# L2's attention layer: stores in two parts, one running maximum, and diagonals by ScalarE

## The chip, the cores and the metric

One Trainium2 chip, one of its cores. The metric is the device time of one execution in microseconds, and of several runs the median. The engines are named as in the profile: PE (TensorE, with PEld for its weight loads), DVE (VectorE), ACT (ScalarE), POOL (GpSimd) and SP (SyncE, which here only issues transfers).

## What is computed

Four pairs of a graph layer and a feed-forward layer, each added to a residual x of 3125 nodes by 256 features; the graph has 50000 edges. The stages that the change touches most belong to the third graph layer, L2:

```python
def _L2_gnn_ref(feature, src, dst, W_s, W_t, W_attn, W_fc, b_fc):
    proj_s = feature @ W_s.T
    proj_t = feature @ W_t.T
    z = proj_s[src] + proj_t[dst]
    z = jnp.where(z >= 0, z, NEG_SLOPE * z)
    e = (z @ W_attn.T)[:, 0]
    m = jax.ops.segment_max(e, src, num_segments=n)
    e_exp = jnp.exp(e - m[src])
    denom = jax.ops.segment_sum(e_exp, src, num_segments=n)
    alpha = e_exp / denom[src]
    agg = jax.ops.segment_sum(feature[src] * alpha[:, None], dst, num_segments=n)
    return agg @ W_fc.T + b_fc
```

So the softmax is over the edges that leave a node, and the sum over the edges that enter one: two passes over the edges, the first sorted by source, the second by destination.

## The kernel before, in words

The nodes lie in 25 windows (T) of 125 rows (PT), one node per partition. The edges, padded and sorted by window, lie in 415 tiles (NTE) of 128. Each engine runs a hand-written program in order; semaphores (`Mark`, and `Ring` for transfers that take turns) order the engines against each other, and at the end of each stage `K.meet` makes all five wait for one another. The stages of L2 are these.

L2Project makes the projections window by window. SP stores each window into tables in HBM: tabT (257 columns, line 2305) and tabB (386 columns, line 2309), each a transfer of 125 rows. At the end SP waits for the landings (line 2316).

L2Max is the pass by source. POOL gathers one tile of tabT rows per instruction (line 2543), which it may do 16 tiles ahead; a buffer comes free with PE's sum of its tile and with ACT's copy of its last column (line 2598). PE sums into PSUM (lines 2632, 2634); DVE forms the score of each edge (line 2563) and per group of four tiles adds the gathered part to it (line 2571). Then it multiplies the identity by the four score columns (line 2577), which gives four diagonal matrices of 128x128. PE multiplies these by ones, on top of a mask of which edge belongs to which node (lines 2614, 2616, in `lay`), so that a bank holds the scores of a group laid out by node. DVE takes the maximum of each tile and node (line 2547) into TM, negates it (line 2553), and ACT forms the sum of exponentials against it (line 2606) into TS. Once per eight tiles DVE also compares a row of 1024 edge positions with the partition number (line 2493).

L2Combine lies between the passes. TM and TS hold, per node, one maximum and one sum for each of 415 tiles, though a tile belongs to one window only. For each of 25 windows DVE compares the window number of all tiles with it (line 2669), adds that as a penalty and takes the maximum (line 2678, over 415 columns), ACT forms 415 exponentials (line 2708), and DVE sums them against TS (line 2698). Small DVE steps make the scale and the shift of the normalised features (lines 2673 to 2691), ACT writes them into a row buffer (lines 2714 to 2717), and SP stores them into the last 258 columns of tabB (line 2722), again 125 rows at a time. POOL clears the accumulator of the next stage (line 2660). PE has no part in it.

L2Sum is the pass by destination; its first instruction on POOL is a gather of tabB (line 2756).

The other tables are stored in the same way: tabA in the sort (line 599) and for L1 (line 1862), whose landing SP waits for; tabC in L3Project (line 2933, landing at line 2935), where DVE clears an accumulator at the end (line 2956); and the output (line 3373).

Of the kernel before, what the change touches and what calls it, by code (L numbers as in the profile page):

```python
# [18 lines left out]
D = 256  # L19
T = 25  # L20
# [62 lines left out]
class Kit:  # L83
# [94 lines left out]
    def dma(self, total=1, keep=False, kind="dma"):  # L178
        return self.mark(total, 16, keep, kind)

    def ring(self, slots, total, kind="dma", keep=False):

        return Ring([self.dma((total - r + slots - 1) // slots, keep, kind) for r in range(min(slots, total))])
# [324 lines left out]
class Sort:  # L508
# [8 lines left out]
    def __init__(self, K):  # L517
# [38 lines left out]
        self.tab, self.got = K.ring(4, T), K.dma()  # L556
# [38 lines left out]
    def sync_tables(self, s, edges):  # L595
        K = self.K
        for t in range(T):
            s.wait_ge(*self.stored.n(t + 1))
            s.dma_start(K.tabA[t * PT:(t + 1) * PT, :], self.acc[0:PT, t * D:(t + 1) * D]).then_inc(*self.tab.up(t))
# [566 lines left out]
class Moe:  # L1166


    def __init__(self, K, layer, E, top, F, NT, key, router, rbias, ecols, shared=False, post=None, side=None):
# [88 lines left out]
        if layer == 0:  # L1258
            self.table = K.W(T * D)
            self.c_norm, self.c_out = K.mark(T), K.ring(4, T)  # L1260
# [597 lines left out]
    def table_sync(self, s):  # L1858
        K = self.K
        for t in range(T):  # L1860
            s.wait_ge(*self.c_norm.n(t + 1))
            s.dma_start(K.tabA[t * PT:(t + 1) * PT, :], self.table[0:PT, t * D:(t + 1) * D]).then_inc(*self.c_out.up(t))
# [381 lines left out]
class L2Project(Project):  # L2244
# [4 lines left out]
    def __init__(self, K, source):  # L2249
# [23 lines left out]
        self.got, self.tabT, self.tabB = K.dma(), K.ring(self.RT, T), K.ring(self.RS, T)  # L2273
# [23 lines left out]
    def sync(self, s):  # L2297
# [4 lines left out]
        for i in range(T + 3):  # L2302
            if i < T:
                s.wait_ge(*self.score.n(i + 1))
                s.dma_start(K.tabT[i * PT:(i + 1) * PT, :], self.whole(i, 1)).then_inc(*self.tabT.up(i))
            if i >= 3:
                t = i - 3
                s.wait_ge(*self.part[2].n(2 * t + 1))
                s.dma_start(K.tabB[t * PT:(t + 1) * PT, 0:DP], self.psB[0:PT, t % self.RS * DP:(t % self.RS + 1) * DP]).then_inc(*self.tabB.up(t))
# [195 lines left out]
class L2Max:  # L2505
# [49 lines left out]
    def vector(self, v):  # L2555
# [3 lines left out]
        for k in range(NTE):  # L2559
# [5 lines left out]
            if k % 4 == 3 or k == NTE - 1:  # L2565
# [76 lines left out]
class L2Combine:  # L2642


    def __init__(self, K, proj):
# [3 lines left out]
        self.pen = [g(EP) for _ in range(4)]  # L2649
        self.ex = [g(EP) for _ in range(3)]  # L2650
        self.jk = g(EP)
        self.row = [g(D + 2) for _ in range(4)]
        self.scale, self.shift = g(32), g(32)
        self.maxes, self.expo, self.sums = K.mark(T), K.mark(T), K.mark(T)
        self.scales, self.filled = K.mark(T), K.mark(T)
        self.cleared = K.mark(1)
        self.out = K.ring(4, T)

    def gpsimd(self, g):
        g.memset(self.pr.acc[0:PT, :], 0.0).then_inc(*self.cleared.up)  # L2660
        g.wait_ge(*self.cleared.n(1))

    def vector(self, v):
        K, pr, own = self.K, self.pr, self.K.own_v
        for i in range(T + 4):
            if i < T:
                if i >= 4:
                    v.wait_ge(*self.expo.n(i - 3))
                v.tensor_scalar(self.pen[i % 4][0:PT, 0:NTE], K.wtS[0:PT, 0:NTE], float(i), -BIG, ALU.not_equal, ALU.mult).then_inc(*own.up)
            if 4 <= i:  # L2670
                t = i - 4
# [1234 lines left out]
```

## Time and profile before

| | us |
|---|---|
| median of 3 runs | 5704.95 |
| lowest and highest of them | 5691.93, 5708.81 |
| the profiled execution, time | 5709.71 |
| its span, first to last instruction | 5707.6 |
| L2Max, first gather to last exponential | 2786.0 to 3340.7 |
| L2Combine, up to the first gather of L2Sum | 3340.9 to 3402.85 |
| busy in the span: PE, DVE, ACT, POOL | 4446.5, 3468.2, 2051.0, 3554.7 |

Times in rows are microseconds from the start of the span unless marked ns. A tile name such as small or big is the memory that the buffers were cut from; "bank" is PSUM. "x25" is a count of instructions, and what stands behind "|" or in brackets is idle time of that engine before them and what ended it. In the tables by stretch the order is: from and to, length, busy time of PE, PEld, DVE, ACT and POOL with counts, the granted clock of PE as a share of full speed (1.00 is 2.4 GHz, 0.50 is 1.2), the share of the 16 DMA engines that was busy, and GB/s.

### The profile page before, as it was taken

To read this page: it belongs to the slowest core of one execution; us is meant where nothing else is said; L and a number is where in the kernel's file an instruction comes from. 1 tells how busy PE (TensorE), PEld (TensorE's weight loads), DVE (VectorE), ACT (ScalarE), POOL (GpSimd) and SP (SyncE) were. 2 spreads that over 40 slices of the span, in tenths; PEclk is the share of its full clock that TensorE was granted. 3 is DMA by queue.
4 is the path that set the end of the run, shared out by engine and by line. 5 is a ranking of instruction groups with operands and counts; after the bars stand their busy time and mean duration, and the time that the engine had idled before them with its cause. 6 is when DMAs were issued, how large, how long until landed. Compare 5 with 4: busy or idle time off the path is not lost. (4 is left out here: it accounts for less than half of the span.)

```text
span 5707.6 us, 86269 instructions
## 1 busy us (share of the span) xinstructions
PE 4446.5 (78%) x19702; PEld 2875.8 (50%) x19702; DVE 3468.2 (61%) x12030; ACT 2051.0 (36%) x7165; POOL 3554.7 (62%) x3817
## 2 busy tenths in 40 slices
PE   6958787799867777387599848888696788877768
PEld 4423337699723335344355526666594333345536
DVE  8957543310167774524466668887415688867775
ACT  7900002233333334023333345554243455544331
POOL 7777775677567773674677737775124477756620
PEclk8955658899856668556899979999696899999978
DMA  2543346688567771142344438886473588876500
GB/s 61 161 153 103 105 102 195 230 274 273 193 182 205 207 202 21 53 106 72 106 128 128 127 99 278 287 278 193 149 211 110 152 231 231 229 186 190 157 19 23
DMA packets 531878, 914.75 MB, mean 160 GB/s; under 512 B 99410, under 2 KB 381985, under 8 KB 522945
## 3 DMA queue, kind: packets, MB, share of 16 engines
q0 software_dynamic: 161600, 449.89, 28.3%
q1 hardware_dynamic: 309354, 330.73, 18.6%
q10 hardware_dynamic: 60438, 128.64, 7.3%
q8 instruction: 186, 3.05, 0.2%
q14 instruction: 300, 2.45, 0.1%
HBM read 739.18 MB, written 169.72 MB: 159 GB/s over the span
## 5 line engine op out<-in xcount | busy, mean ns | idle before, releaser
L1132 PE MATMUL bank<-small 128*125 128x256 f32 x1660 | 818.5, 614 | 302.2 <-DVE small L1099 163.8
L1080 POOL DMA_INDIRECT small<-tabA,idxD x830 | 803.4, 968 | 267.2 <-issue 181.3
L1132 PEld LDWEIGHTS bank<-small 128*125 128x125 f32 x1660 | 372.9, 277 | 747.0 <-issue 409.1
L3018 POOL DMA_INDIRECT small<-tabC,idxD x415 | 410.3, 989 | 190.9 <-SPq L202 64.8
L914 POOL DMA_INDIRECT recs<-pkS,rowS x391 | 385.6, 986 | 229.5 <-issue 98.2
L2756 POOL DMA_INDIRECT big<-tabB,idxD x415 | 395.0, 952 | 198.4 <-issue 88.9
L2543 POOL DMA_INDIRECT big<-tabT,idxS x415 | 411.7, 992 | 138.5 <-issue 107.5
L1111 DVE TENSOR_TENSOR big<-big,bank 125x256 f32 x830 | 347.6, 419 | 240.9 <-PE bank L1132 224.6
L1665 DVE COPY small<-bank 128x256 f32<-128x256 f32 x176 | 74.8, 425 | 680.5 <-PE bank L1720 680.5
L3096 PE MATMUL bank<-big,cst 128*125 128x512 f32 x830 | 427.2, 596 | 0.5 <-ACT big L3083 0.5
L1709 PE MATMUL bank<-small,big 128*128 128x128 f32 (+1 forms) x3040 | 400.2, 288 | 0.0
L1720 PE MATMUL bank<-big 128*128 (+1 forms) x1520 | 390.9, 404 | 3.1 <-issue 3.1
L1709 PEld LDWEIGHTS bank<-small,big 128*128 128x128 f32 (+1 forms) x3040 | 368.1, 196 | 19.0 <-issue 18.9
L3082 ACT ACTIVATE big<-cst,small 128x128 f32<-128x128 f32 x830 | 286.9, 393 | 241.0 <-DMA small<-tabC,idxD 237.8
L1633 POOL DMA_INDIRECT small<-tabA,small x176 | 169.0, 960 | 311.4 <-PE bank L1696 160.6
L3177 POOL TENSOR_TENSOR big<-big 128x256 f32<-128x256 f32 x415 | 245.7, 630 | 144.8 <-ACT big L3238 144.8
L3264 PE MATMUL bank<-big,small 128*125 128x260 f32 x830 | 268.1, 423 | 65.5 <-DVE big L3217 60.8
L2406 PE MATMUL bank<-big,small 125*128 x1245 | 214.4, 281 | 133.6 <-DMA big<-tabB,idxD 72.0
L1720 PEld LDWEIGHTS bank<-big 128*128 128x128 f32 (+1 forms) x1520 | 286.8, 199 | 52.0 <-issue 21.5
L1749 ACT ACTIVATE big<-bank,small 128x128 f32<-128x128 f32 (+1 forms) x760 | 220.8, 367 | 245.9 <-PE bank L1709 241.8
L1121 ACT ACTIVATE small<-small 128x256 f32<-128x256 f32 x415 | 172.9, 417 | 373.4 <-DVE small L1104 373.4
L3065 DVE TENSOR_REDUCE small<-bank 125x4 f32<-125x512 f32 x415 | 284.1, 685 | 0.0
(495 smaller groups left out, 10440.9 us busy)
## 6 DMA issues: line engine op xcount, KB each, us to landing
big<-in_L_w ACTq DMA_DIRECT2D x56, 1024.0 KB
small<-eaS SPq DMA_DIRECT2D x415, 128.0 KB
eaS<-small SPq DMA_DIRECT2D x415, 128.0 KB, 2.8
big<-eaS SPq DMA_DIRECT2D x415, 128.0 KB, 3.1
big<-in_L2f_w ACTq DMA_DIRECT2D x64, 512.0 KB
big<-rowsD SPq DMA_DIRECT2D x104, 256.0 KB, 3.9
ytab<-small ACTq DMA_DIRECT2D x176, 128.0 KB
big<-rowsS SPq DMA_DIRECT2D x52, 256.0 KB
```

What stands on the lines that cost most here:

```text
L914: g.indirect_dma_start(out=K.recs, out_offset=bass.IndirectOffsetOnAxis(ap=K.rowS[:, c:c + 1], axis=0), in_=K.pkS[:, c:c + 1], in_offset=N ...
L1080: g.indirect_dma_start(out=self.gb[k % self.RG], out_offset=None, in_=K.tabA, in_offset=row_index(K.idxD, k)).then_inc(*self.got.up(k))
L1111: v.tensor_tensor(rows, rows, K.bank[k % 4][0:PT, 0:D], ALU.add).then_inc(*self.added.up)
L1132: p.matmul(self.K.bank[k % 4][0:PT, 0:D], self.oh[k % self.RO][:, 0:PT], self.gb[k % self.RG], start=True, stop=True).then_inc(*self.summe ...
L1709: m = p.matmul(self.hidden(k, hf)[0:hc, j * 128:j * 128 + 128], w1[:, c * F + f * 128:c * F + f * 128 + hc], xT[:, c, :], start=(c == 0), ...
L1720: m = p.matmul(K.bank[6 + k % 2][:, 0:D], self.hT[k % self.RT][0:hc, f * 128:(f + 1) * 128], K.big[0:hc, bass.ds(where + f * D, D)], start ...
L2543: g.indirect_dma_start(out=self.rows(k)[:, 0, :], out_offset=None, in_=K.tabT, in_offset=row_index(K.idxS, k)).then_inc(*self.got.up(k))
L2756: g.indirect_dma_start(out=self.gb[k % self.RB], out_offset=None, in_=K.tabB, in_offset=row_index(K.idxD, k)).then_inc(*self.got.up(k))
L3018: g.indirect_dma_start(out=self.gb[k % self.RG], out_offset=None, in_=K.tabC, in_offset=row_index(K.idxD, k)).then_inc(*self.got.up(k))
L3065: v.tensor_reduce(self.tm[k % 4][0:PT, 0:4], K.bank[k % L][0:PT, :].rearrange("p (h e) -> p h e", h=4), AXX, ALU.max).then_inc(*self.top.up)
L3082: a.activation(self.diagonals(k, h, 1), K.ident, ACT.Copy, scale=gb[:, D + h:D + h + 1])
L3096: p.matmul(b, K.ones[:, 0:PT], self.dg[k % self.RD], start=False, stop=True).then_inc(*self.field.up)
```

## The change

Stores: the new `store_rows` issues rows 0 to 111 and rows 112 to 124 as two transfers, and the marks that count landings count 32 in place of 16. It is used for tabA (both), tabT, tabB, tabC and the output.

L2Max: the diagonals of a group are made by ACT, with four copies of the identity that are scaled by a score column, in place of DVE's one multiplication. ACT does this after it has freed the buffers of the next group and before the exponentials.

L2Combine is written anew. The tiles of a window stand side by side in sorted order, so DVE runs one maximum along the 415 tiles that starts again where the window changes; its value at the last tile of each window is the window's maximum. PE picks these values by transposes and matmuls with 0/1 matrices (`of`: tile belongs to window, made by POOL; `last`: it is the last of it). PE spreads the maxima back over the tiles, DVE subtracts, ACT forms one exponential over 415 columns, DVE multiplies by TS, and PE sums by window in the same way. The normalised features are written by DVE and ACT, three and two of each five windows, and stored five windows at a time.

```diff
+def store_rows(s, dst, src, landed):
+    s.dma_start(dst[0:112], src[0:112]).then_inc(landed[0], 16)
+    s.dma_start(dst[112:PT], src[112:PT]).then_inc(landed[0], 16)
...
@@ L2Max.vector
                 if g >= self.LR:
                     self.highest(v, g - self.LR)
-                if g >= self.RD:
-                    v.wait_ge(*self.field.n(g - self.RD + 1))
-                v.wait_ge(*self.whole.n(g + 1))
-                v.tensor_tensor(self.dg[g % self.RD][:, 0:n * 128].rearrange("p (t e) -> p t e", e=128), K.ident.unsqueeze(1).broadcast_to([128, n, 128]),
-                                pr.Ecol[:, four].unsqueeze(2).broadcast_to([128, n, 128]), ALU.mult).then_inc(*self.spread.up)
@@ L2Max.scalar
+            if 1 <= g <= NG:
+                self.spread_terms(a, g - 1)
             if g >= self.LE:
...
+    def spread_terms(self, a, g):
+        K, pr = self.K, self.pr
+        if g >= self.RD:
+            a.wait_ge(*self.field.n(g - self.RD + 1))
+        a.wait_ge(*self.whole.n(g + 1))
+        for i in range(self.size(g)):
+            k = 4 * g + i
+            ins = a.activation(self.dg[g % self.RD][:, 128 * i:128 * i + 128], K.ident, ACT.Copy, scale=pr.Ecol[:, k:k + 1])
+        ins.then_inc(*self.spread.up)
@@ L2Combine
+    NB, P, WR = 4, 104, D + 2
...
     def gpsimd(self, g):
+        K = self.K
+        g.tensor_scalar(self.of[0:T, 0:NTE], K.wtS[0:T, 0:NTE], K.lane[0:T, 0:1], None, ALU.is_equal).then_inc(*self.marked.up)
         g.memset(self.pr.acc[0:PT, :], 0.0).then_inc(*self.cleared.up)
...
     def vector(self, v):
...
+        v.memset(self.flag, 1.0).then_inc(*own.up)
+        v.wait_ge(*own.all)
+        v.tensor_tensor(self.flag[:, 1:NTE], K.wtS[:, 1:NTE], K.wtS[:, 0:NTE - 1], ALU.not_equal).then_inc(*self.flagged.up)
+        v.wait_ge(*self.flagged.n(1))
+        v.tensor_scalar(self.reset, self.flag, -4.0 * BIG, None, ALU.mult).then_inc(*own.up)
+        v.wait_ge(*own.all)
+        v.tensor_tensor_scan(out=self.run[0:PT, 0:NTE], data0=self.reset[0:PT, 0:NTE], data1=TM, initial=-4.0 * BIG,
+                             op0=ALU.add, op1=ALU.max).then_inc(*self.ran.up)
+        v.wait_ge(*self.marked.n(1))
+        v.tensor_tensor(self.last[0:T, 0:NTE], self.of[0:T, 0:NTE], self.flag[0:T, 1:NTE + 1], ALU.mult).then_inc(*self.turned.up)
...
+        v.tensor_tensor(self.less[0:PT, 0:NTE], TM, K.bank[4][0:PT, 0:NTE], ALU.subtract).then_inc(*self.lowered.up)
+        v.wait_ge(*self.expo.n(1))
+        v.tensor_tensor(self.ex[0:PT, 0:NTE], self.ex[0:PT, 0:NTE], TS, ALU.mult).then_inc(*self.weighed.up)
...
+        for t in range(T):
+            if t % 5 % 2 == 0:
+                v.tensor_scalar(self.rows[0:PT, t, 0:D], K.xt(t), self.scale[0:PT, t:t + 1], self.shift[0:PT, t:t + 1],
+                                ALU.mult, ALU.add).then_inc(*self.filled_v.up)
...
+    def tensor(self, p):
...
+        p.wait_ge(*self.turned.n(1))
+        for b in range(self.NB):
+            n, at = self.size(b), b * 2 * T
+            p.transpose(K.bank[0][0:n, at:at + T], self.of[0:T, b * P:b * P + n], K.ident[0:T, 0:T])
+            m = p.transpose(K.bank[0][0:n, at + T:at + 2 * T], self.last[0:T, b * P:b * P + n], K.ident[0:T, 0:T])
...
+        for b in range(self.NB):
+            n = self.size(b)
+            m = p.transpose(K.bank[(1, 7)[b // 2]][0:n, b % 2 * 128:b % 2 * 128 + PT], self.run[0:PT, b * P:b * P + n], K.ident[0:PT, 0:PT])
...
+        for b in range(self.NB):
+            n, at = self.size(b), b * 2 * T + T
+            p.matmul(K.bank[3][0:T, 0:PT], self.pick[0:n, at:at + T], self.runT[0:n, 128 * b:128 * b + PT], start=(b == 0), stop=(b == self.NB - 1))
+        for b in range(self.NB):
+            n, at = self.size(b), b * 2 * T + T
+            m = p.matmul(K.bank[2][0:PT, 0:T], self.runT[0:n, 128 * b:128 * b + PT], self.pick[0:n, at:at + T], start=(b == 0), stop=(b == self.NB - 1))
...
+        p.matmul(K.bank[4][0:PT, 0:NTE], self.MT[0:T, 0:PT], self.of[0:T, 0:NTE], start=True, stop=True).then_inc(*self.wide.up)
...
     def sync(self, s):
...
+        for q in range(5):
+            s.wait_ge(*self.filled_a.n(2 * q + 2))
+            s.wait_ge(*self.filled_v.n(3 * q + 3))
+            store_rows(s, K.tabB.rearrange("(t p) d -> p t d", p=PT)[:, 5 * q:5 * q + 5, DP:DP + D + 2],
+                       self.rows[0:PT, 5 * q:5 * q + 5, :], self.out.up)
```

The matmul and transpose groups each wait for the copies out of PSUM before them and raise a mark behind them; the last two groups (four transposes of `ex`, four matmuls by `of`) have the form of those shown.

## Rows read from the trace of the kernel before

**Rows 1.** By stretch: length, busy us of PE, PEld, DVE, ACT, POOL

```profile
2900.00:3000.00 100.00, 90.28 (x290) 52.21 (x288) 65.38 (x246) 31.31 (x172) 76.41 (x78) 1.00 0.49 129
...
3341.00:3403.00 62.00, 0.00 (x0) 0.00 (x0) 52.30 (x225) 33.07 (x100) 5.51 (x2) 0.50 0.18 52
```

**Rows 2.** The page's group of L2Max's gathers; busy us, mean ns

```profile
L2543 POOL DMA_INDIRECT big<-tabT,idxS x415 | 411.7, 992 | 138.5 <-issue 107.5
```

**Rows 3.** Line 2543: ns min/median/max, and one cause of idling

```profile
L2543 POOL DMA_INDIRECT big<-tabT,idxS x415: 942/946/1447, 2786.0 to 3322.9; - x139
...
  PE bank L2634: 16.1, 53
```

**Rows 4.** Timeline in L2Max: start, length; a lengthened gather, then an undisturbed one

```profile
2999.53 0.68 DVE L2577 TENSOR_TENSOR small<-cst,big 128x512 f32<-128x512 f32 x1
2999.58 1.45 POOL L2543 DMA_INDIRECT big<-tabT,idxS  x1 [0.30 <-issue]
...
3005.08 0.94 POOL L2543 DMA_INDIRECT big<-tabT,idxS  x1 [0.30 <-issue]
...
3005.58 0.68 DVE L2577 TENSOR_TENSOR small<-cst,big 128x512 f32<-128x512 f32 x1
```

**Rows 5.** Groups of instructions by line in L2Combine: count, busy us, mean ns

```profile
L2708 ACT ACTIVATE small<-small,big 125x415 f32<-125x415 f32 x25 | 16.0, 641 | 23.2 <-DVE big L2687 23.2
L2678 DVE CUSTOM_DVE_ANT_0 small<-big,small 125x415 f32<-125x415 f32 x25 | 14.8, 591 | 0.9
L2717 ACT ACTIVATE small<-X,small 125x256 f32<-125x256 f32 x25 | 14.6, 586 | 0.0
...
L2687 DVE TENSOR_SCALAR big<-big 125x1 f32<-125x1 f32 x25 | 3.9, 154 | 0.9
```

**Rows 6.** Timeline at the start and at the end of L2Combine

```profile
3340.90 5.96 DVE L2669 TENSOR_SCALAR small<-wtS 125x415 f32<-125x415 f32 x2 [3.18 <-ACTq L204]
3340.92 5.43 POOL L2660 MEMSET big<- 125x6400 f32 x1 [17.06 <-PEq L204]
...
3402.85 0.95 POOL L2756 DMA_INDIRECT big<-tabB,idxD  x1 [56.49 <-SPq L202]
```

**Rows 7.** What SP's queue waited for: us in total, times, longest

```profile
SPq L2935 <- DMA tabC<-big: 7.4, 1, 7.4
SPq L2316 <- DMA tabB<-big: 6.0, 3, 2.7
...
SPq L1009 <- DMA tabA<-big: 4.5, 1, 4.5
```

**Rows 8.** By stretch; the last two numbers are DMA share and GB/s

```profile
4470.00:4475.00 5.00, 5.00 (x29) 4.17 (x28) 2.03 (x5) 3.22 (x10) 0.00 (x0) 1.00 0.35 107
...
3412.00:3436.00 24.00, 19.56 (x126) 13.79 (x125) 18.04 (x81) 11.10 (x32) 17.08 (x19) 0.93 0.89 294
```

**Rows 9.** Timeline at the end of L3Project

```profile
4476.34 5.47 DVE L2956 MEMSET big<- 125x6500 f32 x1 [1.30 <-issue]
```

**Rows 10.** Timeline in L3Max: two ACT copies of a scaled diagonal

```profile
4699.62 0.69 ACT L3082 ACTIVATE big<-cst,small 128x128 f32<-128x128 f32 x2 [1.02 <-DMA small<-tabC,idxD]
```

**Rows 11.** Groups by line and shape: POOL's operations and DVE's scan

```profile
L819 POOL TENSOR_SCALAR small<-big 128x125 f16<-128x125 f16 x78 | 59.7, 786 | 10.2 <-DVE big L618 8.6 <-PE bank L719 1.6
...
L1782 POOL TENSOR_TENSOR X<-X,big 125x1280 f32<-125x1280 f32 x5 | 14.4, 2889 | 5.1 <-ACT big L1892 5.0
...
L425 DVE TENSOR_TENSOR_SCAN big<-big 128x391 f16<-128x391 f16 x50 | 48.9, 1017 | 0.0
```

**Rows 12.** PE at half clock: a stretch, then two rows of the timeline

```profile
2785.00:2788.00 3.00, 1.95 (x8) 1.52 (x8) 0.00 (x0) 0.13 (x1) 1.66 (x2) 0.50 0.12 26
...
2796.90 2.08 PE L2632 MATMUL bank<-big,cst 128*128 128x512 f32 x2 [9.13 <-DVE big L2493]
...
2797.92 0.34 PEld L2634 LDWEIGHTS bank<-big 125*128 125x128 f32 x1 [0.52 <-issue]
```

**Rows 13.** What the exponentials of line 2606 waited for (us, times)

```profile
  DVE big L2553: 44.5, 46
```

More of the change, by code:

```diff
@@ L176, in mark, with dma, ring @@
         return m
[L178 to L183, printed above, removed]
+    def dma(self, total=1, keep=False, kind="dma", parts=1):
+        return self.mark(total, 16 * parts, keep, kind)
+    def ring(self, slots, total, kind="dma", keep=False, parts=1):
+        return Ring([self.dma((total - r + slots - 1) // slots, keep, kind, parts) for r in range(min(slots, total))])
     def close(self):
@@ L2648, in __init__, with size @@
         K.w_at, K.g_at = proj.w_end, 0
[L2649 to L2652, printed above, removed]
+        self.flag, self.reset, self.run, self.of, self.last = g(EP), g(EP), g(EP), g(EP), g(EP)
+        self.less, self.ex = g(EP), g(EP)
+        self.pick, self.runT, self.exT = g(self.NB * 2 * T), g(self.NB * 128), g(self.NB * 128)
+        self.M, self.MT = g(32), g(128)
         self.scale, self.shift = g(32), g(32)
-        self.maxes, self.expo, self.sums = K.mark(T), K.mark(T), K.mark(T)
-        self.scales, self.filled = K.mark(T), K.mark(T)
+        self.rows = K.big[:, 0:T * self.WR].rearrange("p (t c) -> p t c", c=self.WR)
+        self.flagged, self.marked, self.turned, self.picks = K.mark(1), K.mark(1), K.mark(1), K.mark(1)
+        self.ran, self.flipped, self.back_a, self.back_v = K.mark(1), K.mark(1), K.mark(1), K.mark(1)
+        self.most, self.kept, self.wide = K.mark(1), K.mark(1), K.mark(1)
+        self.lowered, self.expo, self.weighed = K.mark(1), K.mark(1), K.mark(1)
+        self.flipped2, self.back_a2, self.back_v2, self.summed = K.mark(1), K.mark(1), K.mark(1), K.mark(1)
+        self.scaled, self.filled_a, self.filled_v = K.mark(1), K.mark(10), K.mark(15)
         self.cleared = K.mark(1)
-        self.out = K.ring(4, T)
+        self.out = K.dma(5, parts=2)
+    def size(self, b):
+        return min(self.P, NTE - b * self.P)
     def gpsimd(self, g):
+        K = self.K
+        g.tensor_scalar(self.of[0:T, 0:NTE], K.wtS[0:T, 0:NTE], K.lane[0:T, 0:1], None, ALU.is_equal).then_inc(*self.marked.up)
         g.memset(self.pr.acc[0:PT, :], 0.0).then_inc(*self.cleared.up)
@@ new lines, in scalar @@
+    def scalar(self, a):
+        K, pr, w = self.K, self.pr, 128 * self.NB // 2
+        a.wait_ge(*self.picks.n(1))
+        a.activation(self.pick[0:self.P, :], K.bank[0][0:self.P, 0:self.NB * 2 * T], ACT.Copy).then_inc(*K.own_a.up)
+        a.wait_ge(*self.flipped.n(1))
+        a.wait_ge(*K.own_a.all)
+        a.activation(self.runT[0:self.P, w:2 * w], K.bank[7][0:self.P, 0:w], ACT.Copy).then_inc(*self.back_a.up)
+        a.wait_ge(*self.most.n(1))
+        a.activation(self.rows[0:PT, :, D], K.bank[2][0:PT, 0:T], ACT.Copy, scale=-1.0).then_inc(*K.own_a.up)
+        a.activation(self.rows[0:PT, :, D + 1], K.bank[2][0:PT, 0:T], ACT.Copy).then_inc(*K.own_a.up)
+        a.wait_ge(*self.lowered.n(1))
+        a.activation(self.ex[0:PT, 0:NTE], self.less[0:PT, 0:NTE], ACT.Exp).then_inc(*self.expo.up)
+        a.wait_ge(*self.flipped2.n(1))
+        a.activation(self.exT[0:self.P, w:2 * w], K.bank[0][0:self.P, 0:w], ACT.Copy).then_inc(*self.back_a2.up)
+        a.wait_ge(*self.scaled.n(1))
+        a.wait_ge(*K.own_a.all)
+        for t in range(T):
+            if t % 5 % 2:
+                a.activation(self.rows[0:PT, t, 0:D], K.xt(t), ACT.Identity, scale=self.scale[0:PT, t:t + 1],
+                             bias=self.shift[0:PT, t:t + 1]).then_inc(*self.filled_a.up)
@@ L2727 @@
+    def sync(self, s):
+        K = self.K
+        for q in range(5):
[3 more added lines that the diff above has]
+                       self.rows[0:PT, 5 * q:5 * q + 5, :], self.out.up)
+        s.wait_ge(*self.out.all)
 class L2Sum:
@@ L3359, in __init__ @@
         self.w_flip, self.w_turn, self.w_out, self.done = (K.mark(T) for _ in range(4))
-        self.stores = K.ring(8, T)
+        self.stores = K.ring(8, T, parts=2)
     def sync(self, s):
@@ L3732, in _ @@
             K.meet(p, "p")
+            l2_comb.tensor(p)
             K.meet(p, "p")
```

116 lines of the change are left out of this document (49 added, 67 removed).

## Prediction

> **What bounds the kernel now.** The kernel is a row of stages, each closed by a meeting of all engines, so a saving inside a stage counts only if it lies on the chain that ends that stage. I read the busy time by stage first. In the diagonal stage (L2's first pass, L2Max, 2786 to 3341 us) PE is busy 90% and POOL 77% of a stretch; in the stage of maxima between the passes (L2Combine, 3341 to 3403 us) PE does nothing and DVE is busy nearly throughout [rows 1]. Next the gathers of L2Max: 415 of them, 0.946 us in the median, and what stands before them is only the 0.3 us of issue; even the pauses put down to PE are 16.1 us in 53 cases, again 0.3 us each [rows 2, 3]. So POOL never waits for a free buffer, and L2Max lasts as long as 415 gathers at 0.946 + 0.30 us (517 us) plus their lengthening, a start and a tail. PE's 90% fits into that. The mean gather is 992 ns, though [rows 2], so lengthened gathers cost 415 x 0.046 = 19.1 us of this bound.
>
> The timeline shows by what. A gather that starts just after the DVE multiplication that builds four diagonals (L2577, 0.68 us) takes 1.45 us; it ends late by about the rest of that instruction. When the multiplication starts half a microsecond into a gather, it costs nothing [rows 4]. Going through the whole stage, 30 gathers of this kind are 9.2 us too long; nearly all of the remaining 10 us fall to the wide comparison L2493, which stays. I read this as two engines needing one way into the memory.
>
> L2Combine is DVE work: 25 window tiles with two 415-column reductions of 0.59 us and a comparison each, and small steps between [rows 5]. Its first DVE comparison lasted until POOL's memset of 5.43 us was over, and the first gather of the next stage comes 61.95 us after the start [rows 6].
>
> Last, what SP waits for at the ends of stages: 7.4 us for tabC, three waits of 6.0 us together for tabB, 4.5 us for tabA [rows 7]. While tabC is stored, the DMA engines stand at a share of 0.35, a little over 5 of 16, and move 107 GB/s; in another stretch they move 294 GB/s at 0.89 [rows 8]. A store of 125 rows thus seems to fill five engines and leave eleven idle.
>
> **Part 1, the stores.** Each store becomes two issues of some 0.25 to 0.4 us on SP. The 112 rows can go out over 16 engines. L3Project: landing ends 7.4 us after the last issue; with little queued it should take 2.5 to 3. DVE's memset, which ends at 4481.8, takes over as the last piece [rows 9], so 4.5 us are gained. L2Project: of the 6.0 us about 2.4 (three more issues are added, and index work on DVE stands close behind). The table of L1: of 4.5 us about 2.1. The other stores of the list lie beside work that is longer (in the sort, edge rows are scattered for long after the last table store): nothing. Sum 9 us, bounds 3 and 13. The pages would give the same direction: the Trainium skill, "DMA: Bandwidth & Descriptors", section on why a DMA increments its semaphore by 16, says that a transfer is spread over the largest number up to 16 that divides its outer dimension, 5 for 125, 16 for 112 and 13 for 13. By that rule the trace's share of 0.35 is what five engines and some noise give.
>
> **Part 2, diagonals by ScalarE.** DVE loses 104 multiplications of 0.68 us. DVE was not the bound, so that by itself is nothing. ACT gets 415 copies of 128x128; two in a row take 0.69 us in a later stage of this kernel [rows 10], so a group of four is about 1.3 us. ACT was busy 32 of 100 us, and a group takes some 5.1 us, so it rises to about 58%. Behind the new wait for the sums of group g-1 stand four exponentials and the freeing of the buffers of the next group; those sums are made a group earlier, and the buffers have four groups of slack, so I cost the wait at nothing. If that cover is gone, see the slow rival. PE needs the diagonals of a group only two groups later. What it does bring is the port: the 9.2 us fall away, less what the other comparison may catch instead. I take 8 us; bounds 0 (the comparison takes over all) and 12. At the tail DVE gains 0.55 us and ACT has three copies to do first: nothing.
>
> Against this stands a page: the Trainium skill, "SBUF — State Buffer", section "Who interferes with whom", says that a DVE operation with two SBUF inputs holds only the shared read interface, and infers from it that such an operation does not stall the making of descriptors. By that remark this part would be worth 0 and the sum 30 us; the 1.45 us gather speaks against it, and it is the first rival.
>
> **Part 3, L2Combine.** Removed: all of the 62 us. Added, from the start t0 = 3340.9:
> POOL compares 415 columns before its memset. From 2.89 us for 1280 columns that is 0.94 us, from the 0.79 us of a comparison over 125 columns 2.6 us [rows 11]; I take 1.6. The memset (5.43) then ends at 7.0. DVE's full-width multiplication by -4 BIG is of the kind that lasted as long as the memset did [rows 6], so I let it end 0.4 after it: 7.4. Scan, as 1.0 us for 391 columns [rows 11], and the marks of last tiles, 0.5: 9.0. PE at half clock, since it has been idle (clock 0.50 in the stretch of 62 us [rows 1]): 12 transposes at 0.21 to 0.25 us each, by 8 in 1.95 us [rows 12]: 11.9. Copies out of PSUM with handoff 0.5: 12.4. Eight fp32 matmuls are 16 records; a weight load is 0.34 at this clock, one record of 512 columns 1.04 [rows 12]; eight records with 25-column weights at 0.25 and eight with 125-column weights at 0.34 are 4.7: 17.1. Copy 0.3, the wide matmul (2 x 0.84 + 0.34) 2.0: 19.4. Subtraction 0.59, exponential 0.64, product 0.59 [rows 5] and handoffs: 21.4. Four transposes 1.1, copies 0.5, eight records 3.0: 26.0. Four small DVE steps on 25 columns, where one on a single column is 0.15 [rows 5], about 0.25 each: 27.0. Then 25 tiles are normalised, 15 by DVE and 10 by ACT; at 0.5 us ACT's ten are 5 us (0.586 is the length of one [rows 5], and they overlap a little). The first five are ready at 28.2. From there 25 x 129 KB = 3.2 MB go out; five engines at 107 GB/s make 342 for sixteen, and 294 was seen [rows 8], so 9.5 to 11 us plus 1.5 us of start: 40. Meeting and issue 0.5: 40.5 against 61.95, a gain of 21 us. The chain is serial, so nothing hides it. Bounds: if the memset holds nobody and PE finds its full clock, 5 + 6 us less, gain 32; if each of some 17 handoffs costs 0.3 more and the stores run at 200 GB/s, gain 10.
>
> **The sum.** 9 + 8 + 21 = 38 us. The profiled execution has a span of 5707.6 and a time of 5709.7; its changed counterpart would take 5671.7. It stands 4.8 us above the median of the runs, so the median 5704.95 becomes 5667.
>
> **Rivals.**
> (a) The gathers are not freed: another DVE instruction catches them instead, or the multiplication was not the cause. For it: the comparison L2493 already takes 10 us of lengthening, and its place relative to the gathers may shift. Against: the lengthened gather of [rows 4] fits the end of the multiplication. 9 + 21 = 30 us: 5675.
> (b) The change doesn't do what it says for the stores: the two parts still run at the old rate, for want of HBM writes or because the small part of 13 rows is slow. Then L2Combine's 3.2 MB at 107 GB/s take 30 us after 28.2, which ends near 60: no gain there and none at the other ends, only part 2 remains. 5697, within 0.3% of before. Against: 294 GB/s were moved elsewhere [rows 8].
> (c) L2Combine's chain is slower than summed, at its bound of 10: 9 + 8 + 10 = 27 us: 5678.
> (d) Slower: ACT becomes the clock of L2Max. It works in order, so a late sum holds four copies, four exponentials and the freeing of buffers. If a group took 0.6 us longer than POOL's 5.1, 104 groups cost 62 us against a gain of 30: 5737. It decides from where ACT's work per group (0.2 + 1.3 + 1.4) plus its waits passes 5.1 us, so waits of over 2.2 us per group would be needed; now its exponentials wait for DVE about 1 us in 46 of the 104 groups [rows 13].
>
> **How the numbers follow.** Forecast 0.58, (a) 0.2, (c) 0.13, (b) 0.06, (d) 0.03. The predicted time is the forecast's, 5667. Its bounds add to gains of 13 to 57 us, but not all ends come together; gains of 18 to 53 hold 8 in 10 with (a) and (c) inside: 5652 to 5687. About 0.3%, or 17 us, is what a measurement can tell from no change. Faster by more: 0.91; within: 0.06; slower: 0.03.
>
> **What would show it.** In the changed profile: L2Combine from the last exponential of L2Max to the first gather of tabB some 41 us, with DVE's full-width multiplication ending just after POOL's memset, and the DMA share near 0.9 in its last 10 us; gathers of L2Max with a mean near 970 ns and still only issue pauses; ACT busy about 58% there; the wait for tabC at 2 to 3 us. I am wrong if POOL in L2Max begins to wait for PE or ACT, if the stores show a share of 0.35 again, or if PE's matmuls in L2Combine take twice what rows at half clock say.

## The result, and the profile after

The changed kernel takes 5652.04 us in the median of four runs (5645.28 to 5656.55); the kernel before, run beside it, takes 5701.41 (5691.93 to 5708.81). The ratio is 0.991 with a 95% interval of 0.9897 to 0.9923, so the change is worth 51 us, between 44 and 59, where 38 were forecast. (Gains in us are worked out below in the same way, from the ratio and its interval.) The direction came as forecast, and so did the gains of the diagonals and of L2Combine, nearly step by step. The stores were worth about twice their term, and with that the median stands at the lower edge of the stated range (5652 to 5687).

The profiled execution of after took 5645.28 us, 7 below its median, and that of before 5709.71, 8 above its own. Their difference of 64.4 us therefore overstates the gain, and below I compare stages across several executions where a few us matter.

L2Max first. The page's group of its gathers answers to [rows 2], the one-line view of its gathers to [rows 3], and the stretch of 100 us to the first row of [rows 1] (order: from and to, length, busy PE, PEld, DVE, ACT, POOL, granted clock, DMA share, GB/s):

```profile
L2549 POOL DMA_INDIRECT big<-tabT,idxS x415 | 404.9, 976 | 136.4 <-issue 104.8 <-PE bank L2647 18.0 <-SPq L202 10.3
```

```profile
L2549 POOL DMA_INDIRECT big<-tabT,idxS x415: 942/946/1392, 2770.8 to 3300.9; - x139
```

```profile
2900.00:3000.00 100.00, 89.94 (x292) 53.46 (x293) 56.14 (x221) 53.34 (x250) 76.23 (x79) 1.00 0.48 130
```

The mean gather fell from 992 to 976 ns, with the median where it was. DVE gave up 9 us per 100 and ACT took on 22. POOL's waits before a gather are again 0.3 us each, also the 59 that are put down to PE (18.0 us): ACT did not become the clock. From the first gather to the last are 530.1 us, against 536.9 before. What is left over 946 ns, 12.5 us in all, falls to gathers beside the comparison that builds 1024 edge positions, here one of them:

```profile
3097.74 0.75 DVE L2499 TENSOR_SCALAR big<-big,lane 128x1024 f32<-128x1024 bf16 x1
3097.91 1.39 POOL L2549 DMA_INDIRECT big<-tabT,idxS  x1 [0.31 <-issue]
```

L2Combine next, from the timeline (start, length, engine, line). It now takes 38.2 us, from 3317.90 to 3356.06, against 61.95 [rows 6]:

```profile
3317.90 1.33 POOL L2684 TENSOR_SCALAR small<-wtS,lane 25x415 f32<-25x415 f32 x1 [16.06 <-ACTq L204]
...
3319.02 5.83 DVE L2695 TENSOR_SCALAR small<-small 128x416 f32<-128x416 f32 x1
3319.19 5.42 POOL L2685 MEMSET big<- 125x6400 f32 x1
3324.88 1.02 DVE L2697 TENSOR_TENSOR_SCAN small<-small,big 125x415 f32<-125x415 f32 x1
...
3326.52 0.25 PE L2753 MATMUL bank<-cst,small 25*104 25x25 f32 x1 [13.01 <-DVE small L2700]
...
3329.16 1.83 PE L2765 MATMUL bank<-small 104*25 104x125 f32 x8 [0.61 <-DVE small L2702]
...
3333.17 1.74 PE L2771 MATMUL bank<-small 25*125 25x415 f32 x2 [0.37 <-DVE small L2704]
...
3341.38 5.02 ACT L2744 ACTIVATE big<-X,small 125x256 f32<-125x256 f32 x10 [3.08 <-DVE small L2718]
3341.38 4.93 DVE L2723 TENSOR_SCALAR big<-X,small 125x256 f32<-125x256 f32 x15
3342.53 0.32 SPq L227 DMA_DIRECT2D tabB<-big  x1
...
3356.06 1.03 POOL L2823 DMA_INDIRECT big<-tabB,idxD  x1 [31.45 <-SPq L202]
```

This is the forecast chain: POOL's comparison, the memset beside a DVE multiplication that lasts until it is over, the scan, PE's short blocks with handoffs of 0.4 to 0.6 us between them, the normalising up to 3346.4, beside which the stores begin, and then nearly 10 us in which nothing but the stores runs. Three stretches, from PE's blocks to the end:

```profile
3330.00:3345.00 15.00, 7.47 (x27) 5.20 (x25) 6.37 (x20) 4.85 (x12) 0.00 (x0) 0.50 0.10 29
3345.00:3350.00 5.00, 0.00 (x0) 0.00 (x0) 1.31 (x5) 1.40 (x3) 0.00 (x0) 0.50 1.02 305
3350.00:3356.00 6.00, 0.00 (x0) 0.00 (x0) 0.00 (x0) 0.00 (x0) 0.00 (x0) 0.50 0.72 212
```

PE works at a granted clock of 0.50, its lower level of 1.2 GHz, as it did when idle before. From 3345 to 3350 the stores fill the DMA engines, at 305 GB/s.

Last, what SP waits for (us in total, times, longest), the answer to [rows 7]:

```profile
SPq L202 <- DMA tabB<-big: 3.9, 1, 3.9
...
SPq L2322 <- DMA tabB<-big: 1.9, 2, 1.4
SPq L3002 <- DMA tabC<-big: 1.2, 1, 1.2
SPq L3442 <- DMA out_x<-X: 1.0, 1, 1.0
SPq L1015 <- DMA tabA<-big: 0.9, 1, 0.9
```

The landing of tabC took 7.4 us and now takes 1.2, those of tabB 6.0 and now 1.9, that of tabA 4.5 and now 0.9. The first line is the new stage's own store.

### The profile page after: what moved, and what is told of

Same layout as the page of the kernel before. It is cut to its first block and busy times, and to the rows that moved or that the text cites. A ratio compares the mean times of both kernels' runs of the same rounds, so it can differ in the third digit from the quotient of the medians.

```text
span 5643.2 us, 86482 instructions
## 1 busy us (share of the span) xinstructions
PE 4436.4 (79%) x19744; PEld 2874.0 (51%) x19744; DVE 3377.0 (60%) x11730; ACT 2141.2 (38%) x7496; POOL 3551.8 (63%) x3818
## 5 line engine op out<-in xcount | busy, mean ns | idle before, releaser
L1715 PEld LDWEIGHTS bank<-small,big 128*128 128x128 f32 (+1 forms) x3040 | 367.0, 195 | 19.3 <-issue 19.2
L2569 DVE SCALAR_TENSOR_TENSOR small<-bank,big 128x256 f32<-128x256 f32 x415 | 163.1, 421 | 220.2 <-PE bank L2647 219.8
```

What stands on the lines that cost most here:

```text
L1715: m = p.matmul(self.hidden(k, hf)[0:hc, j * 128:j * 128 + 128], w1[:, c * F + f * 128:c * F + f * 128 + hc], xT[:, c, :], start=(c == 0), ...
```

## The experiments

### Each part alone

Three kernels separate the parts. The first has only the stores, those of the old L2Combine among them (edit: `store_rows` as in the change, and `self.out = K.ring(4, T, parts=2)`, with nothing else changed).

> The kernel before with nothing changed but the stores: each store of 125 rows goes out as 112 and 13 rows, L2Combine's 25 too. Theory (stores): it carries all that was gained ahead of L2Max (15.2 us in the profiles of before and after, where 4.5 were forecast), so the first gather of tabT comes near 2771 and not near 2786 us; L3Project ends some 5 us earlier; the whole is 20 to 28 us faster, near 5677. Rival (chance): what was gained ahead of L2Max beyond the landings is the state of one execution; the first gather comes at 2779 to 2783 and the whole is 9 us faster, near 5692. L2Combine itself stays at 60 to 62 us by both, since DVE sets it.

Measured: 5686.88 us against 5705.92, ratio 0.9965 (0.9951 to 0.998). That is 20 us, with 11 to 28 in the interval. The forecast's 9 lies outside. The first gather of tabT comes at 2772.4 us, where this theory put it; but that place moves by itself (2784.3 in a later trace with all these stores split, 2770.9 in one with none of them), so it proves little.

```profile
SPq L2322 <- DMA tabB<-big: 2.3, 3, 1.1
SPq L2941 <- DMA tabC<-big: 1.8, 1, 1.8
...
SPq L2730 <- DMA tabB<-small: 1.2, 1, 1.2
SPq L3381 <- DMA out_x<-X: 0.9, 1, 0.9
SPq L1015 <- DMA tabA<-big: 0.9, 1, 0.9
```

These are SP's waits in that kernel. L2Max is not shortened: its mean gather is 1002 ns. L2Combine, which the expectation left at 60 to 62 us, is 2.9 us shorter than before, by its own last landing (4.3 us before, 1.2 here).

The second has only the diagonals by ACT (edit: the two hunks on L2Max and `spread_terms`).

> The kernel before with only the diagonals of L2Max moved from DVE to ACT. Theory (way into memory shared by DVE and POOL): the mean gather of tabT falls from 992 to about 977 ns as in the changed kernel, L2Max is 7 to 8 us shorter (first gather to start of L2Combine 547 in place of 555), and the whole is 8 us faster, near 5693. Rival (DVE's time): the mean gather stays at 992 ns and what is gained comes from PE waiting less; or nothing is gained.

Measured: 5700.0 against 5705.92, ratio 0.9987 (0.9978 to 0.9997): 7 us, between 2 and 13. The gathers:

```profile
L2543 POOL DMA_INDIRECT big<-tabT,idxS x415 | 404.3, 974 | 139.0 <-issue 104.5 <-PE bank L2641 18.9 <-SPq L202 12.9
```

Followed through the whole stage, the gathers over 947 ns add up to 11.9 us, 10.3 of them beside the wide comparison, alone or with the neighbour behind it; before it was 19.2. First to last gather is 529.5 us. In eight traces in which DVE makes the diagonals that length is 536.9 to 542.8 us, 539.9 in the mean; in four in which ACT alone works for them it is 530.1, 529.5, 527.8 and 529.4. The groups do not touch, and their means are 10.7 us apart.

The third has only the new L2Combine, with each of its five stores as one transfer of 125 rows:

```diff
-            store_rows(s, K.tabB.rearrange(...)[:, 5 * q:5 * q + 5, DP:DP + D + 2],
-                       self.rows[0:PT, 5 * q:5 * q + 5, :], self.out.up)
+            s.dma_start(K.tabB.rearrange(...)[:, 5 * q:5 * q + 5, DP:DP + D + 2],
+                        self.rows[0:PT, 5 * q:5 * q + 5, :]).then_inc(*self.out.up)
```

> The kernel before with only the new L2Combine, and with its stores of five windows going out as one transfer of 125 rows each. If a store of 125 rows is held to about 107 GB/s, its 3.2 MB take some 30 us from the first store, 24.6 us into the stage, so the stage takes 56 to 58 us, 4 to 6 us less than before; the DMA share is near 0.35 in its last part; the whole is 5 us faster, near 5696. If the new stage is fast by its own and the width of the stores matters little, it takes about 38 us as in the changed kernel and the whole is 24 us faster, near 5677. What L2Sum does tells apart whether its 8 us less come from PE having worked just before it (then they show here too) or not.

Measured: 5705.57 against 5705.92, ratio 0.9999 (0.9989 to 1.0008): 1 us, between a loss of 5 and a gain of 6. The stage takes 57.3 us, 4.7 less than before, and 18 of them are this:

```profile
3385.00:3403.00 18.00, 0.00 (x0) 0.00 (x0) 0.00 (x0) 0.00 (x0) 0.00 (x0) 0.50 0.34 104
```

No engine works, and about two thirds of the time of the 16 DMA engines is unused. The old stage hid its slow stores behind 62 us of DVE work; the new one has made them the bound. So the rewriting of L2Combine gains nearly nothing without the edit of the stores. The share of 0.34 is close to what the Trainium skill, "DMA: Bandwidth & Descriptors", section "Why a DMA increments its semaphore by 16 and not by 1", makes of 125 rows: five engines of sixteen, 0.31.

To close this, the same kernel with only those five stores split (edit: rows 0 to 111 and 112 to 124 as two transfers, and ten landings counted in place of five).

> Only L2Combine is new, and its five stores alone are split into 112 and 13 rows; everything else, the diagonals included, is as before. Theory (the new stage's gain hangs on the rate of its own stores): L2Combine lasts 38 to 39 us in place of 57.3 with whole stores and 61.95 before, with a DMA share of 0.7 to 1.0 after the first store, and the whole is 22 to 25 us faster than before, 5682 to 5685, ratio 0.996. Rival (the stage's gain is given back in L2Sum, since its first gathers then collide with stores or index loads): the stage is as short, but the whole is under 15 us faster.

Measured: 5685.18 against 5708.63, ratio 0.9954 (0.9937 to 0.997), 26 us, between 17 and 36 (the medians are 23.5 apart). The stage lasts from 3340.71 to 3378.98, 38.3 us, 19 less than with whole stores. The rival, that L2Sum gives the gain back, fails for the whole, at 26 us. Something may be given back all the same: first to last gather of L2Sum are 542.6 us in this trace and 532.2 to 541.1 in seven traces with the old L2Combine.

```profile
3340.71 1.33 POOL L2671 TENSOR_SCALAR small<-wtS,lane 25x415 f32<-25x415 f32 x1 [16.17 <-ACTq L204]
...
3378.98 1.03 POOL L2811 DMA_INDIRECT big<-tabB,idxD  x1 [31.55 <-SPq L202]
```

### Is it the multiplication that holds the gathers?

Two kernels put work back on DVE in the changed kernel, at the place of the old multiplication. The first adds the same multiplication, into a buffer that nobody reads:

```diff
+                v.wait_ge(*K.own_v.all)
+                v.wait_ge(*self.whole.n(g + 1))
+                v.tensor_tensor(self.spare...[:, 0:n, :], K.ident.unsqueeze(1).broadcast_to([128, n, 128]),
+                                pr.Ecol[:, four].unsqueeze(2).broadcast_to([128, n, 128]), ALU.mult).then_inc(*K.own_v.up)
```

> The changed kernel with DVE's multiplication of identity by score columns kept as extra work: the same operands and shape, written to a buffer that nothing reads, while ACT makes the diagonals that are used. Theory (way into memory): it catches gathers again, so the mean gather of tabT goes back from 977 to 990 ns or more, the gathers of L2Max take 537 to 543 us in place of 528 to 530, and the whole is 9 to 12 us slower than the changed kernel, near 5662. Rival (DVE's time or the later diagonals count): with ACT making the used ones as in the changed kernel, nothing depends on the extra work; 529 us.

The second adds a maximum over 512 columns of one operand, which lasts as long (676 ns in the median, the multiplication 682) and writes 4 columns where the multiplication writes 512:

```diff
+                v.tensor_reduce(self.spare[:, 0:4], K.cst[:, 0:512].rearrange("p (t e) -> p t e", e=128), AXX, ALU.max).then_inc(*K.own_v.up)
```

> The changed kernel with extra work on DVE of about the same length (some 0.6 us per group) and at the same place, but with one operand in place of two: a maximum over four tiles of constants into a scratch column. Theory (way into memory): an instruction with one operand from this memory doesn't hold up gathers; mean gather stays near 977 ns, the gathers of L2Max take 528 to 531 us, and the whole is that of the changed kernel, 5652. Rival (DVE's time): as slow as with the extra multiplication, 537 to 543 us.

Measured, against 5707.57 of the kernel before: the multiplication 5664.96, ratio 0.9924 (0.9907 to 0.994); the maximum 5659.3, ratio 0.9911 (0.9894 to 0.9927). Against the change's own 0.991 the first costs 8 us and the second 0.6. The intervals reach 9 to 10 us to either side, so these two numbers alone settle nothing. The gathers tell them apart:

```profile
L2550 POOL DMA_INDIRECT big<-tabT,idxS x415 | 409.8, 987 | 136.6 <-issue 106.3 <-PE bank L2652 17.1 <-SPq L202 10.5
```

```profile
L2550 POOL DMA_INDIRECT big<-tabT,idxS x415 | 406.3, 979 | 136.8 <-issue 104.2 <-PE bank L2651 20.1 <-SPq L202 10.7
```

With the multiplication the gathers over 947 ns add up to 17.2 us, 9.9 of them in gathers that began while it ran (counted in this way, the old kernel lost 9.8):

```profile
2920.79 0.68 DVE L2583 TENSOR_TENSOR small<-cst,big 128x512 f32<-128x512 f32 x1
2920.84 1.45 POOL L2550 DMA_INDIRECT big<-tabT,idxS  x1 [0.30 <-issue]
```

With the maximum they add up to 13.7 us, and none of it lies at the added instruction, although 68 gathers began while it ran. So it is not the time that DVE is busy but what the instruction does. Two things differ, the second input and the columns written, and no run here separates them; the wide comparison, with one tensor as input and 1024 columns written, catches gathers too.

As a price the effect is smaller than the first expectation. Its gathers have a mean of 987 ns (990 or more were expected) and take 534.9 us from first to last (537 to 543 expected), with the maximum 979 ns and 531.5 us. That is 4.8 us more than the change's 530.1, under half of the 10.7 above: with the multiplication back, the wide comparison catches less, 7.4 us in place of 12.5.

The Trainium skill, "SBUF — State Buffer", section "Who interferes with whom", has a rule for both: an operation with two inputs in SBUF contends with GpSimd's reads, and a reduction never contends. Its inference that a two-input operation does not hold up descriptor making does not agree with this trace (1.45 us against 0.946).

### The memset in L2Combine

POOL's memset waits until the scan is done, in the changed kernel:

```diff
+        g.wait_ge(*self.ran.n(1))
         g.memset(self.pr.acc[0:PT, :], 0.0).then_inc(*self.cleared.up)
```

> The changed kernel with one wait added: POOL clears the accumulator only after DVE's running maximum. Theory (one of DVE and POOL is shut out): DVE's multiplication by -4 BIG takes 0.4 us in place of 5.83, L2Combine 33 us in place of 38, the whole 5 us less than the changed kernel, near 5647. Rival: the multiplication is slow for another reason and stays near 5.8 us, so the stage stays at 38 us.

The stage goes from 38.2 to 32.4 us, 5.4 of which are what the multiplication no longer loses:

```profile
3330.13 0.45 DVE L2696 TENSOR_SCALAR small<-small 128x416 f32<-128x416 f32 x1
3330.61 1.02 DVE L2698 TENSOR_TENSOR_SCAN small<-small,big 125x415 f32<-125x415 f32 x1
...
3331.70 5.43 POOL L2686 MEMSET big<- 125x6400 f32 x1 [1.35 <-DVE small L2698]
...
3361.45 1.03 POOL L2824 DMA_INDIRECT big<-tabB,idxD  x1 [24.32 <-SPq L202]
```

The same multiplication is 0.45 us here and 5.83 us beside the memset. In the whole this does not show: 5654.5 against 5705.92, ratio 0.9906 (0.989 to 0.9923), beside 0.991 of the change. An effect of 5.8 us, 0.1%, is less than either interval, and L2Sum, which is untouched, lasted 528.9 us in the trace of after and 538.2 in this one, in the others 532 to 543.

### Where the stores gain

First, whether it is the number of DMA engines or the splitting itself: all stores in 115 and 10 rows. By the rule of the Trainium skill that is named above ("DMA: Bandwidth & Descriptors"), the large part goes over five engines.

```diff
-    s.dma_start(dst[0:112], src[0:112]).then_inc(landed[0], 16)
-    s.dma_start(dst[112:PT], src[112:PT]).then_inc(landed[0], 16)
+    s.dma_start(dst[0:115], src[0:115]).then_inc(landed[0], 16)
+    s.dma_start(dst[115:PT], src[115:PT]).then_inc(landed[0], 16)
```

> Only the stores changed, as in the kernel with 112 and 13 rows, but they go out as 115 and 10 rows: again two transfers each. Theory (115 rows go over five engines, as 125 do, and 112 over sixteen): nothing is gained; DMA share near 0.35 while tabC is stored, POOL's waits for edge rows in the sort are 9 to 11 us and not 2, the first gather of tabT comes as late as before (2786 to 2797), the whole is that of the kernel before, 5706, or a few us slower for the extra issues. Rival (any smaller or second transfer helps): near 5687 as with 112 and 13.

Measured: 5706.03 against 5707.57, ratio 0.9997 (0.9987 to 1.0006). SP's waits are 6.1 us for tabC, 5.8 for tabB and 3.1 for tabA. POOL's waits for edge rows in the sort are 10.1 us, as with whole stores. The first gather of tabT came at 2780.1 and not at 2786 or later, without the whole being faster. Two transfers in place of one gain next to nothing; the 112 rows do.

The DMA share while tabC is stored says less than the forecast made of it. Its 25 stores of 127 KB leave one per 1.1 us, as the stage makes them, with whole and with split stores alike, which is some 117 GB/s. Whole stores ran at 107 GB/s and a share of 0.35 there, only a little behind; the changed kernel:

```profile
4410.00:4415.00 5.00, 5.00 (x29) 4.09 (x28) 1.91 (x5) 2.95 (x10) 0.00 (x0) 1.00 0.42 121
```

So the mark of a share of 0.35 could tell little there. The clean comparison is in L2Combine: 0.34 at 104 GB/s with whole stores and no engine at work, and 1.02 at 305 GB/s with split stores.

Then the places. Only the stores at the ends of stages (L1's table, tabT, tabB's first part, tabC and the output), with the sort's and L2Combine's whole:

> The kernel before with the stores of L1's table, tabT, tabB's first 128 columns, tabC and the output split, and those of the sort and of L2Combine whole. Theory (stage ends are worth what the landing waits lose): SP's waits fall as in the version with all stores split, for tabC 7.4 to 1.8, for tabB 6.0 to 2.3, for tabA 4.5 to 0.9, for the output 2.1 to 0.9, which is 14 us, ratio 0.9975, while the wait for L2Combine's store stays at 4.3 us and the sort's edge-row waits at 9 to 11. Rival (the forecast's smaller terms at these ends): 9 us, ratio 0.9984. The other rival (nearly all of the 19 us of the version with all stores split come from sort and L2Combine): under 6 us.

Measured: 5691.35 against 5708.63, ratio 0.9966 (0.9952 to 0.998), 19 us, between 11 and 27.

```profile
SPq L2322 <- DMA tabB<-big: 1.9, 3, 1.0
SPq L2941 <- DMA tabC<-big: 1.2, 1, 1.2
SPq L3381 <- DMA out_x<-X: 1.0, 1, 1.0
SPq L1015 <- DMA tabA<-big: 0.9, 1, 0.9
```

The landings lost 15.0 us (before they were 7.4, 6.0, 2.1 and 4.5). The forecast's 9 us lies outside the interval, and so does the rival with under 6. Not all 15 count: in L2Project the waits for tabB fell by 4.1 us, yet the time from the last scatter to the first gather of L2Max only from 13.4 us (13.4 to 14.0 in six traces with whole stores) to 11.0 (11.0 to 11.7 in seven with split ones). In the same stage another wait went that the forecast had not read. POOL's scatters of edge records (line 914) waited 9.4 us in 14 cases for earlier ones to land, here 1.2 in 4. How much of that counts is open: with whole stores these waits are 6 to 9 us in six traces, but with 115 and 10 rows they were 1.3 us as well, and the time was no shorter.

And only the sort's stores:

> The kernel before with only the sort's ten stores of a slice's 125 scaled rows to L1's table split into 112 and 13 rows. Theory (a transfer waits behind the stores that keep five DMA engines): GpSimd's waits for its edge-row loads in the sort fall from 9 to 11 us (four runs with whole stores) to about 2, L1's first tabA gather starts at 322 to 323 us after the span's start in place of 325 to 332, and the whole is 6 to 7 us faster than before, ratio 0.9988. Rival (the difference between the runs' sorts is chance, and the stores lie beside longer work): edge-row waits 9 to 11 us, first gather 325 to 332, ratio 1.000.

Measured: 5699.62 against 5707.78, ratio 0.9988 (0.9978 to 0.9997), 7 us, between 2 and 13. POOL's waits for its rows of edges did fall: 8.9 us before, and here no more than

```profile
POOL eaS L996 <- DMA wiS<-in_ea: 0.3, 1, 0.3
```

In six traces with these stores whole the waits are 8.0 to 12.4 us, in seven with them split 0.3 to 7.8, 3.0 in the mean. But the expected earlier start did not come. L1's first gather starts at 326.2 us, just as in the trace of before: the scatters themselves were longer by 6.0 us in sum (138.9 against 132.9 for 122 of them). That sum varies by itself, from 132 to 137 us with whole stores and from 132 to 139 with split ones, so no cause is to be read from it. Across traces the first gather starts at 325.3 to 332.3 us with whole stores (six traces, 328.2 in the mean) and at 321.5 to 326.2 with split ones (seven, 323.1); with 115 and 10 rows it is 324.9. So an effect of some 5 us is likely but not shown, but this run's 7 us can't be placed in the sort by its trace. The version with all stores split is only 1 us ahead of the one without the sort's and L2Combine's (20 and 19 us), which leaves the sort 0 to 7.

### A store that the change left whole

ACT stores 75 tiles of 125 rows in the three feed-forward stages (line 1374), and DVE waits for them: 96.9 us in 50 cases before. First in the version with the late memset, then in the kernel before by itself:

```diff
-        a.dma_start(self.K.tabA[i * PT:(i + 1) * PT, :], self.xn[i % self.RN][0:PT, :]).then_inc(*self.x_out.up(i))
+        store_rows(a, self.K.tabA[i * PT:(i + 1) * PT, :], self.xn[i % self.RN][0:PT, :], self.x_out.up(i))
```

> The changed kernel with the late clearing of the accumulator, and with the 75 stores of 125 normalised rows that ACT issues in the feed-forward layers also in parts of 112 and 13 rows. DVE waits 98 us in total for the landing of these stores, 47 of them in the first such layer. Theory (five engines limit these too): those waits fall to under a half, edge rows beside them flow better, and the whole is 5 to 20 us faster than with the late clearing alone, 5635 to 5650. Rival (beside longer work, or ACT's second issue of 0.26 us costs as much): near 5654.

> The kernel before with only ScalarE's 75 stores of 125 rows in L2's feed-forward stage and output split into 112 and 13 rows. Theory (those stores, not the eleven that the change split, hold up the feed-forward chain's loads of small rows): about 20 to 25 us faster than before (ratio 0.996), as the version with both was 24 us faster than the one without, and VectorE's waits for the DMA of small rows into tabA fall from 97 to about 77 us. Rival (they gain only behind the new join stage): ratio 0.999 to 1.000 and waits of 97.

Measured: 5630.42 (5625.94 to 5634.72), ratio 0.9861 (0.9845 to 0.9878), and 5687.6, ratio 0.9967 (0.9955 to 0.998). So one further line is worth 19 us alone (11 to 26), and the version with both is the fastest, 79 us below before (70 to 88), where the late memset alone was 54. With that line alone the wait fell further than expected, to 64 in place of 77; in the version with both it fell from 97 to 76.6, where under a half was expected. The wait, before and with that line alone:

```profile
DVE small L270 <- DMA tabA<-small: 96.9, 50, 9.3
```

```profile
DVE small L276 <- DMA tabA<-small: 64.0, 26, 7.3
```

(The second expectation speaks of one stage; the 75 stores are those of all three.)

## Why the prediction was right or wrong, point by point

**What bounds each stage.** Right as far as it went. Gains came where the forecast placed them, in the lengthened gathers, in the serial L2Combine and in landings that SP waits for; some of the stores' gain may have come elsewhere.

**Part 1, the stores: forecast 9, measured 20 with all of them, and 19 with those at the ends of stages alone.** This is the step that failed. The mechanism held, and its terms were too small. The forecast costed a landing at 2.5 to 3 us behind the last issue; with little queued it took 0.9 to 1.8. From L2Sum's last gather to L3's first are 547.8 to 549.7 us in five traces with whole stores and 540.4 to 543.9 in six with split ones, 5.9 apart in the mean, where 4.5 were forecast; DVE's memset did take over as the last piece, as said:

```profile
4420.43 5.47 DVE L3023 MEMSET big<- 125x6500 f32 x1 [1.30 <-issue]
```

At L1's table 3.6 us of waiting went in place of 2.1, and at the output 1.1, to which the forecast gave nothing. L2Project's 2.4 came as 2.4. Together that is 13.0 us where 9 stood. The rest up to 19 is either the scatters' waits or within the interval of 11 to 27; the runs do not say which.

A second step that failed is the sentence "The other stores of the list lie beside work that is longer ...: nothing". The sort's stores alone gained 7 us (2 to 13), though beside the other stores only 0 to 7 are left for them. The sentence asked whether the store itself is on the path, and not what else uses the DMA engines that it occupies. With whole stores the sort's loads of edge rows keep POOL waiting for 8.9 us, with its own stores split for 0.3, and POOL's scatters in L2Project for 9.4 and about 1. ACT's stores, which are no part of the change, hold DVE for 97 and for 64 us. That such transfers queue behind stores which hold the same five engines is my reading, and no view here shows single engines. The Trainium skill, "DMA: Bandwidth & Descriptors", section "Why a DMA increments its semaphore by 16 and not by 1", says that a transfer issued by SP or ACT takes the lowest-numbered engines of the sixteen. The sort agrees with this reading, with waits of 10.1 us at 115 and 10 rows; the scatters do not, with 1.3 us there.

**Part 2, diagonals by ACT: forecast 8, measured 7 (2 to 13), and 10.7 by the length of L2Max.** Right, in mechanism too: the multiplication holds gathers and a reduction of its length does not, shown by putting each back; that it holds them by its second input is not shown. The wide comparison took over only some of what was freed (9.4 us before, 12.5 after), so the rival (a) is out. Four of ACT's copies take 1.26 us where 1.3 were taken, and ACT is busy 53% where 58% were said. Its new waits for DVE and PE are 16.9 us in the whole stage, 0.16 per group, far from the 2.2 us per group of the slow rival (d).

**Part 3, L2Combine: forecast 40.5 us, measured 38.2.** Right, and nearly step by step. Scales are ready 23.5 us after the start where 27.0 were summed: POOL's comparison is 1.33 (1.6 taken), transposes are issued 0.09 us apart rather than one by one, and the eight fp32 records took 1.8 us a block, so 3.7 where 4.7 stood. From the first issue to the next stage's first gather 12.3 us were forecast and 13.5 measured; SP's last issue ends at 3351.9, and the last landing comes 4 us behind it, with the DMA engines full. The forecast of rival (b), that whole stores would take the gain away, was measured as the third kernel: 57.3 us for a sum that ended near 60. Its premise, that split stores stay slow, did not come true.

**The sum.** By parts measured alone: stores at stage ends 19, the sort 0 to 7, diagonals 7 to 11, L2Combine with its own stores 24 by its length. That is 50 to 61, beside 51 (44 to 59) for the whole. The forecast's 38 lacked 10 us or more in the stores and some 3 in L2Combine.

**What stays open.** Where the sort's gain ends up, and how much POOL's scatter waits in L2Project count, and with them some 6 us of the stores' 19; and whether a gather is held by the multiplication's second input or by the columns that it writes.

## What to carry to other kernels

Ask of a transfer how many DMA engines it can spread over, even where nobody waits for it: 125 rows ran at 104 GB/s, and in 112 and 13 rows at 305. With little queued, a landing that a stage waits for took 0.9 to 1.8 us here, and not half of what it was; behind 3.2 MB of stores it took 4. An edit that shortens a chain is worth what the next resource allows: the new L2Combine gained 1 us (-5 to 6) with slow stores and 26 (17 to 36) with fast ones, so two edits that look separate may have to be summed as one. Then search the kernel for the same pattern elsewhere: the one line that the change left alone was worth 19 us, as much as all the stores that it split (20).

## What the runs showed of the hardware

- A DVE multiplication of 128x512 with two inputs in SBUF lengthened a gather of POOL from 0.95 to 1.45 us if the gather started just behind it, and lengthened some 30 of 415 gathers in all; a reduction of the same length with one input and 4 columns written lengthened none of the 68 that began while it ran.
- A DVE multiplication of 128x416 from SBUF to SBUF took 0.45 us alone and 5.83 us beside POOL's memset of 5.42 us: it ended only when the memset had.
- Splitting a store is not what helps: 115 and 10 rows gained nothing (ratio 0.9997) and 112 and 13 rows 20 us. SP pays 0.30 and 0.40 us for the two issues where no queue is full.
- First to last gather of L2Sum, which no run changed, took 529 to 543 us from trace to trace, and the sort's 122 scatters 132 to 139 us: a single trace tells stage lengths no better than that.
